# Separate products for two scan steps, folds in four column groups, and a respread schedule in a four-layer selective-scan kernel

## The chip, the cores and the metric

The kernel runs on one core of a Trainium2 chip. The metric is the device time of one launch in microseconds (us). Names of engines: PE is TensorE, DVE is VectorE, ACT is ScalarE, POOL is GpSimd, SP is SyncE, whose queue starts nearly all DMA copies here. The host does no arithmetic; it only rearranges the weights.

## What is computed

Four layers follow each other on x of 8 images, 64 x 64 pixels, 96 channels. Each layer projects up to 2 x 192 channels, convolves, runs a selective scan over the L = 4096 pixels in K directions (4, 4, 4 and 1), sums the directions, gates, and projects down to 96. The scan of a layer is, for every image, direction, channel d and state n (16 of them):

```python
dts, Bs, Cs = jnp.split(x_dbl, ...)            # small projections of u
delta = softplus(dts @ dt_proj_w + bias)
dA = exp(delta * A[d, n])
h  = dA * h + (delta * u) * B[n]               # along the 4096 pixels
y  = sum over n of h * C[n]   ;   y += D * u
```

## The kernel before

**Tiling.** Two images are worked on together: 2 x 192 channels are three tiles (`TILES`) of 128. The sequence is cut into chunks of `CH` = 1024 pixels; a layer has K x 4 x 4 chunks, so 64, 64, 64 and 16, together 208. A chunk has 3 tiles x 16 steps = 48 steps. A step is one scan instruction of 128 partitions x 1024 pixels: the partitions hold 32 channels x 4 states (a "quad"). Two steps are a unit (both halves of 64 channels, same states), four units are a pair of channel groups, eight units are a tile. The loop body (`BODY_CHUNKS` = 2) holds two chunks, 48 units, written out.

**A unit on five engines.** PE spreads the four B rows over the partitions into PSUM (`fill_b`, L897 to L913: two bf16 matmuls with `pick`, into slot 0 alone). DVE multiplies them with du = delta x u (`multiply`, L1046 to L1058: one instruction of 2 x 1024, which reads slot 0 twice and writes both slots), then scans twice (`scan`, L1060 to L1084, decay from SBUF, product from the slot). ACT makes the decays, exp(A x delta), two steps ahead (`decay_of`, L1103), and saves the last state of each unit (`save`, L1125). POOL multiplies both states by C (`gate`, L1274), and PE adds the four states of each channel into `psy` (`reduce`, L970 to L991: four matmuls with the 128 x 32 matrix `fold`). In three units of eight (`POOL_UNITS` = 2, 5, 7) POOL makes the product (`multiply`, L1298, into `made`) and ACT writes the decay into the slot instead; DVE only scans there. I call these P units and the other five m units, so that a tile is m m P m m P m P.

**What a tile needs from elsewhere.** While tile T is scanned, delta and du of tile T + 1 are made. PE projects (`project_delta`), ACT forms the softplus in parts (`parts`, `exponential`, `logarithm`, `correction`), PE sums the four terms (`add_up`), ACT copies the sum into `delta` (`take_delta`, L1168, signal `delta_ready`), and POOL multiplies it by u into `du` (`delta_u`, L1287, signal `du_ready`). SP then spreads both over the partitions, 8 DMA copies of 128 KB for each pair of channel groups (`spread_pair`, L782 to L790), into rings of three (`delta4`) and two (`du4`) buffers. The first product of each tile on DVE waits until all 8 copies of du of the tile's first pair have landed (L1052, L1053).

**The order of the work is written by hand.** Tables of step numbers (L66 to L78) say in which step, counted by n = 0 to 15 in a tile for PE and ACT, or in which unit, 0 to 7, for POOL and SP, each of these jobs stands. Each engine takes its instructions strictly in order, and so does SP's queue (`after_gate`, L807 to L833, and `chunk_work`). In `after_gate` a unit's order on SP is: the y store; in the units that load B or C, a wait for that unit's gate, then 4 copies for C (units 8 to 11 and 20 to 23 of a chunk of 24) and 4 for B (P units); then the spreads whose unit it is. Every chunk is prepared a chunk ahead (`load`, `store_rows`, `load_flat`, `store_split`, `load_bc`). Once a tile ACT copies `psy` to `ybuf` (`copy_y`, L1192) and SP stores it (`store_y`, L798).

Of the kernel before, what the change touches and what calls it, by code (L numbers as in the profile page):

```python
# [60 lines left out]
H_RING, DECAY_RING, DELTA_RING, DU_RING, B_RING, MADE_RING = 4, 3, 3, 2, 2, 2  # L61
AHEAD, REDUCE_LAG = 2, 2
FLAT = 2 * NS * CH // P


DELTA_AT = (0, 1)  # L66
PARTS_AT, EXP_AT, LOG_AT, CORRECTION_AT, TAKE_AT = 2, 3, 4, 5, 8
SUM_AT = (4, 4, 5, 5, 6, 6, 7, 7)
COPY_Y_AT = 4
XDBL_AT = [(0, 10), (0, 10), (0, 11), (0, 12), (0, 13), (0, 14)]  # L70
SAVE_AT = [(0, 12), (0, 15)]
HI_AT, REST_AT, MID_AT, LESS_MID_AT, LO_AT = (1, 9), (1, 10), (1, 11), (1, 12), (1, 13)

DU_AT, Y_STORE = 4, 1
# [525 lines left out]
def scan_stage(nc, kind, T, W, useq, neg_a, yseq, bcdram, splitdram):  # L600
# [29 lines left out]

    def filled(v):

        return v + 1 - sum(w <= v for w in on_pool)

    def by_vector(s):
# [3 lines left out]
    def pair_of(v):  # L639

        return v // QUADS
# [31 lines left out]
    with ExitStack() as ctx:  # L673
# [32 lines left out]
        state = sb("state", [P, 2, TILES * NS])  # L706
        slots = ctx.enter_context(nc.psum_tensor("slots" + W["tag"], [P, 2, CH], F32))
        slot = [slots[:, j, :] for j in range(2)]
        psc = ctx.enter_context(nc.psum_tensor("psc" + W["tag"], [P, CH], F32))
# [19 lines left out]
        with nc.Block() as block:  # L729
            @block.sync  # L730
            def _(sp):
# [65 lines left out]

                def store_y(i, C0, T_):  # L798

                    q, t = T_ // TILES, T_ % TILES  # L800
                    sp.wait_ge(sem["y_copied"], C0 * TILES + (T_ + 2))
                    here = chunk_and_direction(i, q)[0]
                    if backward(q):
                        here = here + SEQS[kind] * PAIRS * NCH
                    sp.dma_start(yseq[here, t], ybuf[:]).then_inc(sem["y_stored"], 16)

                def after_gate(i, C0, v):  # L807
# [24 lines left out]
                    if n == DELTA_OUT_AT[1]:  # L832
                        spread_delta(2 * T_ + 3)  # L833

# [45 lines left out]
                sp.wait_ge(sem["y_stored"], 16 * (NC * TILES + 2))  # L880
                sp.wait_ge(sem["x_full"], 80 * (NC + 1))
# [14 lines left out]
            def _(pe):  # L896
                def fill_b(C0, v, first=False):  # L897

                    body, v = v // BU, v % BU
                    q = v // UNITS  # L900
                    if v in on_pool:
                        return
                    S = (C0 + body * BODY_CHUNKS) * STEPS + 2 * v
                    if v % UNITS == 0:
# [4 lines left out]
                    rows_of = batch_of(v) * QUADS + v % QUADS  # L909
# [26 lines left out]
                def add_up(A, term, a):  # L936


                    if term == 0 and a == 0:
                        pe.wait_ge(sem["relu_ready"], A + 1)  # L940
                        pe.wait_ge(sem["abs_ready"], A + 1)
                    if term == 1 and a == 0:
                        pe.wait_ge(sem["log_ready"], A + 1)
                    if term == 2 and a == 0:
                        pe.wait_ge(sem["excess_ready"], A + 1)
                    if term == 3 and a == 0:
                        pe.wait_ge(sem["exp_ready"], A + 1)
                    mm = pe.matmul(psc[:, HALF[a]], T["ident"][:, :],  # L948
                                   (relu, log, excess, ex)[term][:, HALF[a]], start=(term == 0), stop=(term == 3),
                                   skip_group_check=True)  # L950
                    if term == 3 and a == HALVES - 1:
                        mm.then_inc(sem["summed"], 1)
# [17 lines left out]
                def reduce(C0, v):  # L970
# [6 lines left out]
                    if v % TILE_UNITS == SKIP_AT:  # L977

                        q, t = v // UNITS % BODY_CHUNKS, v // TILE_UNITS % TILES
                        order = slice(None, None, -1) if backward(q) else slice(None)  # L980
                        for cols in HALF:
                            pe.matmul(psy[:, cols], dd[q][:, t, :], u[q][:, t, order][:, cols], start=False, stop=False,  # L982
                                      skip_group_check=True)
                    first = 2 * GROUP * (pair_of(v) % 2)
                    for cols in HALF:
# [24 lines left out]
                pe.wait_ge(sem["pick_in"], 16)  # L1010
                fill_b(0, 0, first=True)
                with pe.Fori(0, NC // BODY_CHUNKS) as i:
                    C0 = i * BODY_CHUNKS
                    for s in range(BS):
                        if s % 2 == 0:
                            fill_b(C0, s // 2 + 1)
                        q, t, n = place(s)
                        after = s // NS + 1
                        if n in DELTA_AT:
                            a = DELTA_AT.index(n)  # L1020
                            if a == 0 and t == 0:
                                psc_free(C0 * TILES + s // NS)
                            if a == 0 and t == 2:
                                pe.wait_ge(sem["split_lo"], C0 + (q + 2))
                            project_delta(C0 + (q + (t > 0)), after // TILES % BODY_CHUNKS, after % TILES, a)
                        for j, at in enumerate(SUM_AT):
# [18 lines left out]
            def _(dve):  # L1045
                def multiply(C0, body, v):  # L1046
# [4 lines left out]
                    j = pair_of(v)  # L1051
                    if v % QUADS == 0 or v % QUADS == 1 and v - 1 in on_pool:  # L1052
# [38 lines left out]
                with dve.Fori(0, G) as g:  # L1091
                    with dve.Fori(0, per_g) as half:
                        body = g * per_g + half
                        C0 = body * BODY_CHUNKS
                        for v in range(BU):
                            if v not in on_pool:
                                multiply(C0, body, v)
                            scan(C0, body, 2 * v, g)
# [3 lines left out]
            def _(act):  # L1102
                def decay_of(i, s):  # L1103
# [15 lines left out]
                    else:  # L1119
                        act.wait_ge(sem["h_ready"], S + (H_START - DECAY_RING + 1))  # L1120
                        dst = decay[s % DECAY_RING][:]
                    act.activation(dst, delta4[j % DELTA_RING][:, s % 2, :], ACT.Exp, scale=na[q][:, k:k + 1])\  # L1122
                        .then_inc(sem["decay_ready"], 1)
# [68 lines left out]
                def copy_y(C0, T_, q):  # L1192
# [3 lines left out]

                    act.wait_ge(sem["y_stored"], C0 * (16 * TILES) + 16 * (T_ + 1))
                    order = slice(None, None, -1) if backward(q) else slice(None)
                    act.copy(ybuf[:], psy[:, order]).then_inc(sem["y_copied"], 1)


                act.sem_inc(sem["state_saved"], H_RING)

                act.sem_inc(sem["y_stored"], 32)

# [648 lines left out]
```

## Time and profile before

| | us |
|---|---|
| median of 3 runs | 35931.14 (35928.1 to 35933.79) |
| the profiled execution | 35929.24 |
| its span in the trace | 35927.5 |
| DVE busy | 32944.5 (92%) |
| POOL busy | 30835.7 (86%) |
| PE busy | 25878.4 (72%) |
| ACT busy | 19018.1 (53%) |

The span is the time from the first to the last instruction of the profiled execution; "busy" is the time in which an engine had an instruction at work. The stretches of lower use in the trace, between the four scans, are the merging and expanding stages of the layers, which the diff leaves as they are. In the times of the trace, us count from the span's start.

### The profile page before, as it was taken

To read this page: it belongs to the slowest core of one execution; us is meant where nothing else is said; L and a number is where in the kernel's file an instruction comes from. 1 tells how busy PE (TensorE), PEld (TensorE's weight loads), DVE (VectorE), ACT (ScalarE), POOL (GpSimd) and SP (SyncE) were. 2 spreads that over 40 slices of the span, in tenths; PEclk is the share of its full clock that TensorE was granted. 3 is DMA by queue.
4 is the path that set the end of the run, shared out by engine and by line. 5 is a ranking of instruction groups with operands and counts; after the bars stand their busy time and mean duration, and the time that the engine had idled before them with its cause. 6 is when DMAs were issued, how large, how long until landed. Compare 5 with 4: busy or idle time off the path is not lost. (4 is left out here: it accounts for less than half of the span.)

```text
span 35927.5 us, 322721 instructions
## 1 busy us (share of the span) xinstructions
PE 25878.4 (72%) x73032; PEld 8083.4 (22%) x73032; DVE 32944.5 (92%) x14881; ACT 19018.1 (53%) x23286; POOL 30835.7 (86%) x7804
## 2 busy tenths in 40 slices
PE   5777777777766777777777766777777777766777
PEld 2222222222222222222222222222222222222224
DVE  5999999999977999999999977999999999976993
ACT  4555555555534555555555534555555555534551
POOL 1999999999961999999999951999999999964994
PEclk7888888888888888888888888888888888887886
DMA  4666666666675666666666675666666666675665
GB/s 154 176 175 175 177 176 178 176 176 176 176 223 168 177 176 175 177 176 179 176 177 178 176 219 167 177 177 175 176 177 176 178 176 176 177 222 181 176 176 149
DMA packets 2423696, 6402.41 MB, mean 178 GB/s; under 512 B 703824, under 2 KB 875728, under 8 KB 2411728
## 3 DMA queue, kind: packets, MB, share of 16 engines
q1 hardware_dynamic: 2421968, 6387.69, 67.0%
q14 instruction: 1659, 13.59, 0.1%
q8 instruction: 69, 1.13, 0.0%
HBM read 2986.75 MB, written 764.47 MB: 104 GB/s over the span
## 5 line engine op out<-in xcount | busy, mean ns | idle before, releaser
L1283 POOL TENSOR_TENSOR h<-h,c 128x2048 f32<-128x2048 f32 x4992 | 20774.7, 4182 | 242.8 <-DVE h L1083 150.5
L1083 DVE TENSOR_TENSOR_SCAN h<-decay,state,slots 128x1024 f32<-128x1024 f32 x6240 | 14306.8, 2335 | 120.4 <-ACT state L1227 9.3
L988 PE MATMUL psy<-h,t_fold 128*32 128x512 f32 x40000 | 10449.2, 672 | 6.1 <-POOL h L1283 5.9
L1122 ACT ACTIVATE decay<-delta,na 128x1024 f32<-128x1024 f32 x6248 | 7115.4, 1146 | 3014.3 <-DVE h L1083 2775.0
L1079 DVE TENSOR_TENSOR_SCAN h<-slots,state,made 128x1024 f32<-128x1024 f32 x3744 | 8551.7, 2327 | 108.3 <-ACT slots L1122 106.1
L1304 POOL TENSOR_TENSOR made<-du,b 128x2048 f32<-128x2048 f32 x1872 | 7823.4, 4179 | 669.4 <-DMA b<-bcdram 669.4
L911 PE MATMUL slots<-bc,pick 96*128 96x512 bf16 x6248 | 2327.4, 461 | 7905.6 <-DVE h L1079 6853.2
L1056 DVE TENSOR_TENSOR slots<-du,slots 128x2048 f32<-128x2048 f32 x3120 | 7165.4, 2297 | 706.9 <-PE slots L911 298.6
L1122 ACT ACTIVATE slots<-delta,na 128x1024 f32<-128x1024 f32 x3744 | 4166.0, 1114 | 5010.9 <-DVE h L1083 5009.4
L988 PEld LDWEIGHTS psy<-h,t_fold 128*32 128x32 f32 x40000 | 2202.4, 120 | 7785.7 <-issue 7522.8
L1296 POOL TENSOR_TENSOR du<-delta,u 128x1024 f32<-128x1024 f32 x628 | 1478.0, 2353 | 2356.3 <-ACT delta L1176 2356.3
L911 PEld LDWEIGHTS slots<-bc,pick 96*128 96x128 bf16 x6248 | 371.4, 101 | 10707.3 <-DVE h L1079 8558.5
L1130 ACT COPY state<-h 128x2 f32<-128x2 f32 x4992 | 923.8, 185 | 2300.2 <-DVE h L1083 1356.7
L948 PE MATMUL psc<-relu,t_ident 128*128 128x512 f32 x2512 | 1932.8, 915 | 9.2 <-ACT ex L1146 9.2
L919 PE MATMUL psc<-u,wx 128*96 128x512 f32 x2544 | 1647.5, 785 | 202.2 <-DMA bdt<-in_bdt 201.2
L982 PE MATMUL psy<-u,dd 128*128 128x512 f32 x2496 | 1758.5, 846 | 0.0
L1176 ACT COPY delta<-psc 128x1024 f32<-128x1024 f32 x628 | 636.5, 1014 | 1567.7 <-PE psc L948 1567.7
L948 PE MATMUL psc<-log,t_ident 128*128 128x512 f32 x2512 | 1414.7, 692 | 51.5 <-ACT log L1159 51.5
L929 PE MATMUL psc<-dts,wdt 32*128 32x512 f32 x2512 | 1436.2, 696 | 0.9 <-ACT dts L1210 0.9
L948 PE MATMUL psc<-excess,t_ident 128*128 128x512 f32 x2512 | 1181.9, 592 | 0.0
L948 PE MATMUL psc<-ex,t_ident 128*128 128x512 f32 x2512 | 1180.4, 592 | 0.0
L1693 POOL TENSOR_TENSOR tn<-tn,zc 128x1536 f32<-128x1536 f32 x96 | 350.9, 3655 | 920.4 <-ACT tn L1572 920.4
(111 smaller groups left out, 20168.8 us busy)
## 6 DMA issues: line engine op xcount, KB each, us to landing
delta<-delta SPq DMA_DIRECT2D x10048, 128.0 KB, 2.6
du<-du SPq DMA_DIRECT2D x10048, 128.0 KB, 3.0
b<-bcdram SPq DMA_DIRECT2D x7520, 128.0 KB, 2.8
c<-bcdram SPq DMA_DIRECT2D x6720, 128.0 KB, 2.9
u<-useq SPq DMA_DIRECT2D x212, 1536.0 KB, 6.9
yseq<-ybuf SPq DMA_DIRECT2D x624, 512.0 KB, 2.7
ya<-yseq SPq DMA_DIRECT2D x420, 512.0 KB, 4.9
yb<-yseq SPq DMA_DIRECT2D x360, 512.0 KB, 5.9
```

The costliest lines, as they stand in the source:

```text
L911: mm = pe.matmul(slot[0][:, cols], pick[:, rows_of, :], bc[q % 2][:, cols], start=True, stop=True)
L919: mm = pe.matmul(psc[0:96, HALF[a]], wx[q][:, s, :], u[q][:, s, HALF[a]], start=(s == 0), stop=(s == TILES - 1))
L948: mm = pe.matmul(psc[:, HALF[a]], T["ident"][:, :], (relu, log, excess, ex)[term][:, HALF[a]], start=(term == 0), stop=(term == 3), skip_g ...
L982: pe.matmul(psy[:, cols], dd[q][:, t, :], u[q][:, t, order][:, cols], start=False, stop=False, skip_group_check=True)
L988: mm = pe.matmul(psy[rows, cols], T["fold"][:, :], h[v % H_RING][:, c, cols], start=(v % QUADS == 0), stop=(v % QUADS == QUADS - 1), skip_ ...
L1056: dve.tensor_tensor(slots[:, ::-1, :], du4[j % DU_RING][:, ::-1, 1:], slots[:, 0:1, :].broadcast_to((P, 2, CH)), ALU.mult)\
L1079: dve.tensor_tensor_scan(out, slot[s % 2][:, order], made[p % MADE_RING][:, s % 2, order], first, ALU.mult, ALU.add).then_inc(sem["h_ready ...
L1083: dve.tensor_tensor_scan(out, decay[s % DECAY_RING][:, order], slot[s % 2][:, order], first, ALU.mult, ALU.add).then_inc(sem["h_ready"], 1)
L1122: act.activation(dst, delta4[j % DELTA_RING][:, s % 2, :], ACT.Exp, scale=na[q][:, k:k + 1])\
L1283: pool.tensor_tensor(both[:, :, 0:CH], both[:, :, 1:], c4[g][:, order].unsqueeze(1).broadcast_to((P, 2, CH)), ALU.mult)\
L1296: pool.tensor_tensor(du[:], delta[:, 1:], u[q][:, t, :], ALU.mult).then_inc(sem["du_ready"], 1)
L1304: pool.tensor_tensor(made[k % MADE_RING][:], du4[j % DU_RING][:, :, 1:], b4[k % B_RING][:].unsqueeze(1).broadcast_to((P, 2, CH)), ALU.mult)\
```

## The change

B is filled into both PSUM slots (two tensors now), two matmuls for each step; DVE makes one product of 1024 for each step, and waits in it only for `b_full` (and du). PE's jobs between the folds stand on odd steps, with the order of the sum's terms changed. The folds of one unit go to four 32-wide column groups: the two halves of the 1024 pixels now lie in different partitions of `psy`, and the two pairs of channel groups in its two banks. `copy_y` and `store_y` follow that layout (two DMA copies in place of one). The sum for delta is taken in step 10 in place of 8, POOL forms du in unit 5 in place of 4, and SP spreads both pairs of delta in unit 4, in front of du (before: the first in unit 3, the second in unit 4 behind du). Later stores and loads of a chunk move by two or three units.

```diff
-DELTA_AT = (0, 1)
-PARTS_AT, EXP_AT, LOG_AT, CORRECTION_AT, TAKE_AT = 2, 3, 4, 5, 8
-SUM_AT = (4, 4, 5, 5, 6, 6, 7, 7)
+DELTA_AT = (1, 1)
+PARTS_AT, EXP_AT, LOG_AT, CORRECTION_AT, TAKE_AT = 2, 3, 4, 5, 10
+SUM_AT = (3, 3, 5, 5, 7, 7, 9, 9)
...
-XDBL_AT = [(0, 10), (0, 10), (0, 11), (0, 12), (0, 13), (0, 14)]
-SAVE_AT = [(0, 12), (0, 15)]
-HI_AT, REST_AT, MID_AT, LESS_MID_AT, LO_AT = (1, 9), (1, 10), (1, 11), (1, 12), (1, 13)
-DU_AT, Y_STORE = 4, 1
+XDBL_AT = [(0, 11), (0, 11), (0, 13), (0, 13), (0, 15), (0, 15)]
+SAVE_AT = [(0, 14), (1, 0)]
+HI_AT, REST_AT, MID_AT, LESS_MID_AT, LO_AT = (1, 10), (1, 11), (1, 12), (1, 13), (1, 14)
+DU_AT, Y_STORE = 5, 1
...
-DELTA_OUT_AT, DU_OUT_AT = (3, 4), (4, 7)
-LOAD_AT, ROWS_STORE_AT, FLAT_AT, SPLIT_STORE_AT, BC_AT = 2, 6, 8, 13, 15
+DELTA_OUT_AT, DU_OUT_AT = (4, 4), (4, 7)
+LOAD_AT, ROWS_STORE_AT, FLAT_AT, SPLIT_STORE_AT, BC_AT = 2, 8, 10, 16, 18
...
+                    if n == DELTA_OUT_AT[0]:
+                        sp.wait_ge(sem["delta_ready"], C0 * TILES + (T_ + 2))
+                        spread_delta(2 * T_ + 2)
+                    if n == DELTA_OUT_AT[1]:
+                        spread_delta(2 * T_ + 3)
                     if n == DU_OUT_AT[0]:
                         sp.wait_ge(sem["du_ready"], C0 * TILES + (T_ + 2))
                         spread_du(2 * T_ + 2)
                     if n == DU_OUT_AT[1]:
                         spread_du(2 * T_ + 3)
-                    if n == DELTA_OUT_AT[0]:
-                        sp.wait_ge(sem["delta_ready"], C0 * TILES + (T_ + 2))
-                        spread_delta(2 * T_ + 2)
-                    if n == DELTA_OUT_AT[1]:
-                        spread_delta(2 * T_ + 3)
...
                     for cols in HALF:
-                        mm = pe.matmul(slot[0][:, cols], pick[:, rows_of, :], bc[q % 2][:, cols],
+                        mm = pe.matmul(slot[s % 2][:, cols], pick[:, rows_of, :], bc[q % 2][:, cols],
                                        start=True, stop=True)
...
-                    first = 2 * GROUP * (pair_of(v) % 2)
-                    for cols in HALF:
+                    bank = HALF[pair_of(v) % 2]
+                    for a, cols in enumerate(HALF):
                         for c in range(2):
-                            rows = slice(first + GROUP * c, first + GROUP * c + GROUP)
-                            mm = pe.matmul(psy[rows, cols], T["fold"][:, :], h[v % H_RING][:, c, cols],
+                            rows = slice(2 * GROUP * a + GROUP * c, 2 * GROUP * a + GROUP * c + GROUP)
+                            mm = pe.matmul(psy[rows, bank], T["fold"][:, :], h[v % H_RING][:, c, cols],
...
                     for s in range(BS):
-                        if s % 2 == 0:
-                            fill_b(C0, s // 2 + 1)
+                        if s % 2 == 1:
+                            fill_b(C0, s - 1 + FILL_LAG)
+                            fill_b(C0, s + FILL_LAG)
...
-                    dve.wait_ge(sem["b_full"], body * filled(BU - 1) + filled(v))
-                    dve.wait_ge(sem["h_ready"], C0 * STEPS + (2 * v + H_START))
...
-                    dve.tensor_tensor(slots[:, ::-1, :], du4[j % DU_RING][:, ::-1, 1:],
-                                      slots[:, 0:1, :].broadcast_to((P, 2, CH)), ALU.mult)\
-                        .then_inc(sem["b_multiplied"], 2)
+                    dve.tensor_tensor(slot[s % 2][:], du4[j % DU_RING][:, s % 2, 1:], slot[s % 2][:], ALU.mult)\
+                        .then_inc(sem["b_multiplied"], 1)
```

## Rows read from the trace of the kernel before

**Rows 1.** The page's costliest groups: those of the scan stages on DVE and POOL
```profile
L1283 POOL TENSOR_TENSOR h<-h,c 128x2048 f32<-128x2048 f32 x4992 | 20774.7, 4182 | 242.8 <-DVE h L1083 150.5
L1083 DVE TENSOR_TENSOR_SCAN h<-decay,state,slots 128x1024 f32<-128x1024 f32 x6240 | 14306.8, 2335 | 120.4 <-ACT state L1227 9.3
...
L1079 DVE TENSOR_TENSOR_SCAN h<-slots,state,made 128x1024 f32<-128x1024 f32 x3744 | 8551.7, 2327 | 108.3 <-ACT slots L1122 106.1
L1304 POOL TENSOR_TENSOR made<-du,b 128x2048 f32<-128x2048 f32 x1872 | 7823.4, 4179 | 669.4 <-DMA b<-bcdram 669.4
...
L1056 DVE TENSOR_TENSOR slots<-du,slots 128x2048 f32<-128x2048 f32 x3120 | 7165.4, 2297 | 706.9 <-PE slots L911 298.6
...
L1296 POOL TENSOR_TENSOR du<-delta,u 128x1024 f32<-128x1024 f32 x628 | 1478.0, 2353 | 2356.3 <-ACT delta L1176 2356.3
```
**Rows 2.** Timeline of DVE over one tile, second of its chunk (start, length, operation, count)
```profile
7032.27 2.30 DVE L1056 TENSOR_TENSOR slots<-du,slots 128x2048 f32<-128x2048 f32 x1 [0.19 <-DVE h L1079]
...
7057.80 2.30 DVE L1056 TENSOR_TENSOR slots<-du,slots 128x2048 f32<-128x2048 f32 x1
7060.13 4.58 DVE L1083 TENSOR_TENSOR_SCAN h<-decay,state,slots 128x1024 f32<-128x1024 f32 x2
7064.63 4.57 DVE L1079 TENSOR_TENSOR_SCAN h<-slots,state,made 128x1024 f32<-128x1024 f32 x2
7069.31 2.30 DVE L1056 TENSOR_TENSOR slots<-du,slots 128x2048 f32<-128x2048 f32 x1
...
7080.90 2.30 DVE L1056 TENSOR_TENSOR slots<-du,slots 128x2048 f32<-128x2048 f32 x1 [0.19 <-DVE h L1079]
```
**Rows 3.** The stages' first and last product on DVE, first and third layer (ns min/median/max)
```profile
L1056 DVE TENSOR_TENSOR slots<-du,slots x960: 2295/2297/2298, 803.2 to 10212.8; 128x2048 f32<-128x2048 f32 x192
...
L1056 DVE TENSOR_TENSOR slots<-du,slots x960: 2295/2297/2298, 22381.8 to 31765.8; 128x2048 f32<-128x2048 f32 x192
```
**Rows 4.** Groups by line and shape: DVE's short products with a PSUM operand
```profile
L1395 DVE TENSOR_TENSOR xr<-xr,outp 96x512 f32<-96x512 f32 x128 | 81.6, 678 | 43.0 <-PE outp L1508 43.0
...
L1395 DVE TENSOR_TENSOR xr<-xr,outp 96x256 f32<-96x256 f32 x128 | 44.9, 410 | 22.9 <-PE outp L1508 22.9
```
**Rows 5.** Timeline of ACT in the tile of rows 2, steps 8 to 11
```profile
7059.61 1.01 ACT L1176 COPY delta<-psc 128x1024 f32<-128x1024 f32 x1 [1.67 <-PE psc L948]
...
7064.75 1.12 ACT L1122 ACTIVATE slots<-delta,na 128x1024 f32<-128x1024 f32 x1 [0.79 <-DVE h L1083]
7065.81 0.18 ACT L1130 COPY state<-h 128x2 f32<-128x2 f32 x1
7065.89 2.25 ACT L1122 ACTIVATE decay<-delta,na 128x1024 f32<-128x1024 f32 x2
```
**Rows 6.** Timeline of SP's queue: the third tile of the chunk before, then the tile of rows 2
```profile
6970.75 1.71 SPq L773 DMA_DIRECT2D c<-bcdram  x4
6972.50 4.95 SPq L788 DMA_DIRECT2D du<-du  x8
...
7065.06 4.96 SPq L788 DMA_DIRECT2D delta<-delta  x8
7070.06 5.03 SPq L788 DMA_DIRECT2D du<-du  x8
7075.14 5.11 SPq L788 DMA_DIRECT2D delta<-delta  x8
```
**Rows 7.** The spreading copies of L788, from issue to landing
```profile
DMA to landing us min/median/max: 2.2/2.8/9.1
```
**Rows 8.** PE around a tile's start (timeline), and all of L929 in 4000 us
```profile
6979.62 1.04 PE L911 MATMUL slots<-bc,pick 96*128 96x512 bf16 x2 [6.93 <-DVE h L1079]
...
6987.21 0.61 PE L911 MATMUL slots<-bc,pick 96*128 96x512 bf16 x2 [1.55 <-DVE h L1083]
6987.75 1.98 PE L929 MATMUL psc<-dts,wdt 32*128 32x512 f32 x4
...
L929 PE MATMUL psc<-dts,wdt x328: 587/588/1217, 5025.2 to 8999.0; 32*128 32x512 f32 x164
```

More of the change, by code:

```diff
@@ L629, in place @@
         return s // STEPS, s // NS % TILES, s % NS
-    def filled(v):
-        return v + 1 - sum(w <= v for w in on_pool)
     def by_vector(s):
@@ L706, in scan_stage @@
         state = sb("state", [P, 2, TILES * NS])
-        slots = ctx.enter_context(nc.psum_tensor("slots" + W["tag"], [P, 2, CH], F32))
-        slot = [slots[:, j, :] for j in range(2)]
+        slot = [ctx.enter_context(nc.psum_tensor(f"slot{j}" + W["tag"], [P, CH], F32)) for j in range(2)]
         psc = ctx.enter_context(nc.psum_tensor("psc" + W["tag"], [P, CH], F32))
@@ L804, in store_y @@
                         here = here + SEQS[kind] * PAIRS * NCH
-                    sp.dma_start(yseq[here, t], ybuf[:]).then_inc(sem["y_stored"], 16)
+                    halves = yseq[here, t].rearrange("(r p) (a f) -> a p r f", r=2, a=HALVES)
+                    for a in range(HALVES):
+                        sp.dma_start(halves[HALVES - 1 - a if backward(q) else a],
+                                     ybuf[2 * GROUP * a:2 * GROUP * a + 2 * GROUP, :].rearrange("p (r f) -> p r f", r=2))\
+                            .then_inc(sem["y_stored"], 16)
                 def after_gate(i, C0, v):
@@ L879, in _ @@
                             chunk_work(i, C0, v)
-                sp.wait_ge(sem["y_stored"], 16 * (NC * TILES + 2))
+                sp.wait_ge(sem["y_stored"], 32 * (NC * TILES + 2))
                 sp.wait_ge(sem["x_full"], 80 * (NC + 1))
@@ L896, in _, with fill_b @@
             def _(pe):
[L897 to L901, printed above, removed]
+                def fill_b(C0, s, first=False):
+                    body, s = s // BS, s % BS
+                    q, t, n = place(s)
+                    if s // 2 in on_pool:
                         return
-                    S = (C0 + body * BODY_CHUNKS) * STEPS + 2 * v
-                    if v % UNITS == 0:
+                    S = (C0 + body * BODY_CHUNKS) * STEPS + s
+                    if t == 0 and n == 0:
                         pe.wait_ge(sem["bc_in"], (C0 + body * BODY_CHUNKS) * 16 + 16 * (q + 1))
@@ L908, in fill_b @@
                         pe.wait_ge(sem["h_ready"], S + (H_START - 1))
-                    rows_of = batch_of(v) * QUADS + v % QUADS
+                    rows_of = batch_of(s // 2) * QUADS + s // 2 % QUADS
                     for cols in HALF:
-                        mm = pe.matmul(slot[0][:, cols], pick[:, rows_of, :], bc[q % 2][:, cols],
+                        mm = pe.matmul(slot[s % 2][:, cols], pick[:, rows_of, :], bc[q % 2][:, cols],
                                        start=True, stop=True)
@@ L942, in add_up @@
                     if term == 1 and a == 0:
+                        pe.wait_ge(sem["exp_ready"], A + 1)
+                    if term == 2 and a == 0:
                         pe.wait_ge(sem["log_ready"], A + 1)
-                    if term == 2 and a == 0:
+                    if term == 3 and a == 0:
                         pe.wait_ge(sem["excess_ready"], A + 1)
-                    if term == 3 and a == 0:
-                        pe.wait_ge(sem["exp_ready"], A + 1)
                     mm = pe.matmul(psc[:, HALF[a]], T["ident"][:, :],
-                                   (relu, log, excess, ex)[term][:, HALF[a]], start=(term == 0), stop=(term == 3),
+                                   (relu, ex, log, excess)[term][:, HALF[a]], start=(term == 0), stop=(term == 3),
                                    skip_group_check=True)
@@ L980, in reduce @@
                         order = slice(None, None, -1) if backward(q) else slice(None)
-                        for cols in HALF:
-                            pe.matmul(psy[:, cols], dd[q][:, t, :], u[q][:, t, order][:, cols], start=False, stop=False,
-                                      skip_group_check=True)
-                    first = 2 * GROUP * (pair_of(v) % 2)
-                    for cols in HALF:
+                        for r in range(2):
+                            chans = slice(2 * GROUP * r, 2 * GROUP * r + 2 * GROUP)
+                            for a, cols in enumerate(HALF):
+                                pe.matmul(psy[2 * GROUP * a:2 * GROUP * a + 2 * GROUP, HALF[r]], dd[q][:, t, chans],
+                                          u[q][:, t, order][:, cols], start=False, stop=False, skip_group_check=True)
+                    bank = HALF[pair_of(v) % 2]
+                    for a, cols in enumerate(HALF):
                         for c in range(2):
-                            rows = slice(first + GROUP * c, first + GROUP * c + GROUP)
-                            mm = pe.matmul(psy[rows, cols], T["fold"][:, :], h[v % H_RING][:, c, cols],
+                            rows = slice(2 * GROUP * a + GROUP * c, 2 * GROUP * a + GROUP * c + GROUP)
+                            mm = pe.matmul(psy[rows, bank], T["fold"][:, :], h[v % H_RING][:, c, cols],
                                            start=(v % QUADS == 0), stop=(v % QUADS == QUADS - 1),
@@ L1010, in _ @@
                 pe.wait_ge(sem["pick_in"], 16)
-                fill_b(0, 0, first=True)
+                for s in range(FILL_LAG):
+                    fill_b(0, s, first=True)
                 with pe.Fori(0, NC // BODY_CHUNKS) as i:
@@ L1014, in _ @@
                     for s in range(BS):
-                        if s % 2 == 0:
-                            fill_b(C0, s // 2 + 1)
+                        if s % 2 == 1:
+                            fill_b(C0, s - 1 + FILL_LAG)
+                            fill_b(C0, s + FILL_LAG)
                         q, t, n = place(s)
                         after = s // NS + 1
[L1019 to L1025, printed above, removed]
+                        for a, at in enumerate(DELTA_AT):
+                            if n == at:
+                                if a == 0 and t == 0:
+                                    psc_free(C0 * TILES + s // NS)
+                                if a == 0 and t == 2:
+                                    pe.wait_ge(sem["split_lo"], C0 + (q + 2))
+                                project_delta(C0 + (q + (t > 0)), after // TILES % BODY_CHUNKS, after % TILES, a)
                         for j, at in enumerate(SUM_AT):
@@ L1045, in _, with multiply @@
             def _(dve):
-                def multiply(C0, body, v):
-                    dve.wait_ge(sem["b_full"], body * filled(BU - 1) + filled(v))
-                    dve.wait_ge(sem["h_ready"], C0 * STEPS + (2 * v + H_START))
-                    j = pair_of(v)
-                    if v % QUADS == 0 or v % QUADS == 1 and v - 1 in on_pool:
+                def multiply(C0, body, s):
+                    q, t, n = place(s)
+                    count = by_vector(s)
+                    dve.wait_ge(sem["b_full"], body * by_vector(BS - 1) + count)
+                    j = pair_of(s // 2)
+                    if s // 2 % QUADS == 0 or s // 2 % QUADS == 1 and s // 2 - 1 in on_pool and s % 2 == 0:
                         dve.wait_ge(du_in[j % DU_RING], body * DU_BODY + du_count(j))
-                    dve.tensor_tensor(slots[:, ::-1, :], du4[j % DU_RING][:, ::-1, 1:],
-                                      slots[:, 0:1, :].broadcast_to((P, 2, CH)), ALU.mult)\
-                        .then_inc(sem["b_multiplied"], 2)
+                    dve.tensor_tensor(slot[s % 2][:], du4[j % DU_RING][:, s % 2, 1:], slot[s % 2][:], ALU.mult)\
+                        .then_inc(sem["b_multiplied"], 1)
                 def scan(C0, body, s, g):
@@ L1096, in _ @@
                             if v not in on_pool:
-                                multiply(C0, body, v)
+                                multiply(C0, body, 2 * v)
+                                multiply(C0, body, 2 * v + 1)
                             scan(C0, body, 2 * v, g)
@@ L1120, in decay_of @@
                         act.wait_ge(sem["h_ready"], S + (H_START - DECAY_RING + 1))
-                        dst = decay[s % DECAY_RING][:]
-                    act.activation(dst, delta4[j % DELTA_RING][:, s % 2, :], ACT.Exp, scale=na[q][:, k:k + 1])\
+                        dst = decay[s % DECAY_RING]
+                    act.activation(dst[:], delta4[j % DELTA_RING][:, s % 2, :], ACT.Exp, scale=na[q][:, k:k + 1])\
                         .then_inc(sem["decay_ready"], 1)
@@ L1195, in copy_y @@
                     act.wait_ge(sem["reduced"], C0 * UNITS + (T_ * TILE_UNITS + H_RING + REDUCE_LAG))
-                    act.wait_ge(sem["y_stored"], C0 * (16 * TILES) + 16 * (T_ + 1))
+                    act.wait_ge(sem["y_stored"], C0 * (32 * TILES) + 32 * (T_ + 1))
                     order = slice(None, None, -1) if backward(q) else slice(None)
-                    act.copy(ybuf[:], psy[:, order]).then_inc(sem["y_copied"], 1)
+                    act.copy(ybuf[:].rearrange("p (r f) -> p r f", r=2),
+                             psy[:].rearrange("p (r f) -> p r f", r=2)[:, :, order]).then_inc(sem["y_copied"], 1)
                 act.sem_inc(sem["state_saved"], H_RING)
-                act.sem_inc(sem["y_stored"], 32)
+                act.sem_inc(sem["y_stored"], 64)
                 act.preload_act_table_set("natural_log_exp_and_others")
```

2 lines of the change are left out of this document (1 added, 1 removed).

## The prediction

> **What bounds the kernel now.** I read first the page's costliest groups, then DVE's timeline over a tile, then what SP's queue, ACT and PE do in that tile. The groups [rows 1] show two engines level in the scans: DVE is busy for 14306.8 + 8551.7 + 7165.4 = 30024 us, POOL for 20774.7 + 7823.4 + 1478.0 = 30076 us. Over 208 x 3 = 624 tiles that is 48.1 and 48.2 us a tile. The first and last product of a scan [rows 3] give the pace: 10212.8 - 803.2, plus 11.6 us for units 6 and 7 behind the last product (7080.90 - 7069.31 in [rows 2]), over 64 chunks is 147.2 us a chunk; the third layer gives 146.8. I take 147.0, or 49.0 us a tile. DVE's idle time stands in front of its products, 706.9 us in all [rows 1], nearly nothing in front of its scans; so DVE is the bound, POOL stands right behind it, and POOL's own largest wait in the loop is for the copies of B.
>
> DVE's idle time is mostly its own. Two scans with no wait between them take 4.58 us for 2 x 2335 ns: the second starts 2.25 us after the first, before the first has ended. A product that waits for the scan in front of it starts 0.10 us late (7064.63 + 4.57 = 7069.20, then 7069.31), and the scan behind a product starts 0.03 us late (7057.80 + 2.30, then 7060.13) [rows 2].
>
> **Part 1: two products for one.** A product of 512 takes 678 ns and one of 256 takes 410 [rows 4], so 1.047 ns an element and some 142 ns fixed. One of 1024 is then 2297 - 1024 x 1.047 = 1225 ns. In the new order no instruction of DVE waits for the one just ahead of it: a scan waits for the product two ahead, a product for `b_full` alone. If products overlap as scans do, by 0.08 us, each costs 1.145 us. A tile is then 10 x 1.145 + 16 x 2.255 = 47.5 us against 49.0: a gain of 1.5 us for DVE, if nothing else stood in the way. A rule speaks against it. The Trainium skill, VectorE: DVE Perf Modes, section on the DRAIN that can't be avoided, says that the next operation doesn't start until the pipeline has emptied, and that semaphores add nothing to that. The scans here disagree with both halves, as the 4.58 us and the 0.10 us above show [rows 2]. Without overlap, a tile is 10 x 1.225 + 16 x 2.335 = 49.6 us; I keep that as the other end.
>
> **Part 2: when delta and du arrive.** This is what decides. Take the tile of [rows 2]. Scan 9, the last of unit 4, ends at 7060.13 + 4.58 = 7064.71. Before, ACT took delta in step 8, at 7059.61, ahead of that scan's end; its late decay(10) stood behind it [rows 5]. Afterwards it takes it in step 10: behind decay(11) and the save of unit 4, which both wait for scan 9, and behind decay(12). These start at 7064.75, 7065.81 and 7065.89; the two decays of the last row take 2.25 us together, so the copy could start at 7066.95 and end 1.01 us later: **3.25 us after scan 9**. (POOL's du, now behind unit 4's gate, is there 4.2 + 2.35 = 6.6 us after scan 9; SP needs it only later.)
>
> SP's queue is then in order: 16 copies of delta, 8 of du. Before, the 8 of du stood in the middle. 24 such copies took 7080.25 - 7065.06 = 15.2 us [rows 6], 0.63 us each, so the last one starts after 14.55 us; it lands 2.8 us later [rows 7]. With 0.1 us for two semaphores, the du of the next tile is there 3.25 + 14.55 + 2.8 + 0.1 = **20.7 us after scan 9**. DVE has 2 x 2.255 + (2 x 1.145 + 2 x 2.255) + 2 x 2.255 = 15.8 us of work until it wants it (before: 7080.90 - 7064.71 = 16.2 us, with du landed at 7070.06 + 4.4 + 2.8 = 7077.3, 3.6 us early). So DVE stands still for about 4.9 us at every tile's first product.
>
> This is a closed ring, so no buffer evens it out: first product, units 0 to 4 (8 x 1.145 + 10 x 2.255 + 0.1 = 31.8 us; before, 7064.71 - 7032.27 = 32.4), then the 20.7 us: **52.5 us a tile**, over DVE's 47.5 and POOL's 48.2.
>
> In a chunk's third tile SP's unit 4 begins with 4 copies of C that wait for the gate of unit 4, 4.2 us after scan 9 (4182 ns, [rows 1]), and take 1.7 us [rows 6]. Delta starts at 5.9 in place of 3.25: **2.7 us more once a chunk**.
>
> **Part 3: PE and ACT at a tile's start.** Before, delta's projection stood behind the fill that waits for scan 0. Now it stands behind the fill that waits for scan 1. PE has two levels: two fills take 0.61 us at the upper (2.4 GHz) and 1.04 us at the lower one (1.2 GHz), the latter after 6.9 us of idle time, and the projection 1.98 us, or twice that (588 to 1217 ns for one record) [rows 8]. At the upper level ACT gets it 0.05 + 0.45 + 1.85 = 2.35 us after scan 1. Relu and Abs (2.1 us) are through at 4.5, decay(4) then waits for scan 2 as before, ends at 5.7, the exponentials run to 7.7, decay(5) to 8.8, and DVE wants it at 2 x 1.145 + 3 x 2.255 = 9.05: no cost. At the lower level the projection is there at 4.5, decay(4) at 7.7 where scan 4 is due at 6.8, decay(5) at 10.8 where it is due at 10.0: 1.8 us in all, and it lies in the ring. DVE's standstill leaves PE without work for some 4 us ahead of this, which makes the lower level as likely as not. I take **1.0 us**, between 0 and 1.8. The fill of slot 1 has only one product as its cover (1.07 us against 0.05 + 1.04): 0.1 us at most, counted at nothing.
>
> **Part 4: the rest.** The folds become cheaper if four column groups work at once, the fills dearer by two matmuls; both hide beside DVE, since PE is idle for a quarter of the span (72% busy on the page). The second y store is one more issue on SP in unit 1, far from unit 4. Moving the x projection frees ACT and DVE of a wait of at most the 106.1 us in all that L1079 waits for ACT [rows 1], and the standstill swallows that. Copies of B for P units stand behind du; they land about 2.6 us into the next tile and POOL's product is needed 13.6 us into it: nothing.
>
> **The sum.** A chunk is 3 x (52.5 + 1.0) + 2.7 = 163.2 us against 147.0, so 16.2 us more; 208 chunks make 3370 us. On the profiled execution of 35929 us that gives 39,300; the median of the runs is 2 us off it.
>
> **Bounds.** Low: no PE term, every copy 0.62 us and the last landing after 2.2: 51.65 us a tile, 157.7 a chunk, 38,150. High: no overlap on DVE (33.5 for 31.8), landing after 3.0, the PE term in full: 56.2 us, 171.4 a chunk, 41,000. All at their high end together is unlikely, so I go to 40,500.
>
> **Rivals.** (1) *Faster:* SP's queue isn't the bound. The 0.63 us for a spreading copy would have to fall to about the 0.43 of a C copy (1.71 us for 4, [rows 6]), since DVE's own pace spreads traffic; then 24 copies take 10.2 us, the ring is 31.8 + 3.25 + 9.8 + 2.8 + 0.1 = 47.75 us and POOL's 48.2 decides. The ring decides from 48.2 us on, that is from 0.45 us a copy. A chunk would be some 146, with a little of POOL's wait for B left: 1 us x 208 gained, **35,720**. Against it: the same copies took 0.62 to 0.64 us each in all four runs of 8 in [rows 6], whatever stood around them. (2) *The fixed cost of a product:* the ring doesn't bind and instructions don't overlap; by the rule above a tile is 49.6 + 10 x 0.03 = 49.9, so 0.9 x 624 = 560 us: **36,490**. It needs the ring's absence too, and the scans speak against the rest. (3) *The folds don't run four at a time,* so that the change doesn't do what it says on PE: 0.85 us a unit of PE time is not gained, and the time stays at my forecast, since nothing waits for it.
>
> **How the numbers follow.** The ring of delta and du sets the pace: 0.91 (with it (3), which has no time of its own). Rival (1), or DVE's gain by another road: 0.05. Rival (2): 0.03. No net effect: 0.01. A difference below 0.2%, 72 us, can't be told from none. Faster 0.05, same 0.01, slower 0.94. The range is the ring's own, cut at the unlikely high end: 38,100 to 40,500.
>
> **What would show it.** Right: DVE's idle time before its products rises from 707 us to some 3,000 or more, one long wait of 4 to 8 us a tile, released by the DMA copies of du; products of about 1225 ns, starting 1.15 us apart; POOL's busy time as before and its waits for DVE's scans much longer; a C, delta, du sequence on SP with no gap in unit 4, delta's first copy 3.3 us after scan 9. Part 3 shows in waits of scans in P unit 2 for ACT. Wrong: tiles under 50 us, du landed before scan 15 ends, or POOL with hardly any idle time.

## The result and the profile after

The changed kernel takes 39814.79 us (median of 4, 39807.08 to 39822.37) against 35932.46 for the kernel before, a ratio of 1.1078 (95% interval 1.1064 to 1.1091). The forecast was 39,300 in a range of 38,100 to 40,500.

DVE's waits over the whole span, from the list of waits (in total, times, longest):

```profile
DVE slot L1062 <- DMA du<-du: 3531.6, 620, 8.8
DVE h L1084 <- ACT slot L1128: 1123.6, 1241, 1.4
...
DVE slot L1062 <- PE slot L911: 250.3, 4, 62.9
```

Before, the largest of DVE's waits in the scan stages came to some 300 us (for fills), of which some 250 lie at the starts of the four stages, as the third line still does (4 times, up to 62.9 us). Now one wait, for du, stands at 620 of 624 tiles and costs 5.7 us each time; a second, of scans in P units for ACT, costs 1.8 us a tile. The costliest groups of the page that answer to [rows 1]:

```profile
L1290 POOL TENSOR_TENSOR h<-h,c 128x2048 f32<-128x2048 f32 x4992 | 20787.4, 4176 | 3358.8 <-DVE h L1088 1892.0
L1088 DVE TENSOR_TENSOR_SCAN h<-decay,state,slot 128x1024 f32<-128x1024 f32 x6240 | 14286.5, 2332 | 0.0
...
L1062 DVE TENSOR_TENSOR slot<-du,slot 128x1024 f32<-128x1024 f32 x6240 | 7427.1, 1217 | 3788.2 <-DMA du<-du 3531.6
...
L1084 DVE TENSOR_TENSOR_SCAN h<-slot,state,made 128x1024 f32<-128x1024 f32 x3744 | 8632.4, 2334 | 1124.4 <-ACT slot L1128 1123.6
...
L991 PE MATMUL psy<-h,t_fold 128*32 128x512 f32 x40000 | 6478.8, 731 | 4.1 <-POOL h L1290 4.1
```

The work itself cost hardly more: products 7427 us busy for 7165, scans as before, folds 6479 for 10449, and DVE is busy for 32816 us in all, for 32945 before. What grew is idle time: 3788 us before DVE's products, 3359 before POOL's gates. DVE's timeline from one standstill to the next, the second tile of a chunk and the start of the third, to be read beside [rows 2]:

```profile
6990.26 2.36 DVE L1062 TENSOR_TENSOR slot<-du,slot 128x1024 f32<-128x1024 f32 x2 [4.78 <-DMA du<-du]
...
7004.67 2.35 DVE L1084 TENSOR_TENSOR_SCAN h<-slot,state,made 128x1024 f32<-128x1024 f32 x1 [0.83 <-ACT slot L1128]
7007.50 2.35 DVE L1084 TENSOR_TENSOR_SCAN h<-slot,state,made 128x1024 f32<-128x1024 f32 x1 [0.47 <-ACT slot L1128]
...
7018.75 4.58 DVE L1088 TENSOR_TENSOR_SCAN h<-decay,state,slot 128x1024 f32<-128x1024 f32 x2
7023.24 4.57 DVE L1084 TENSOR_TENSOR_SCAN h<-slot,state,made 128x1024 f32<-128x1024 f32 x2
...
7043.97 2.36 DVE L1062 TENSOR_TENSOR slot<-du,slot 128x1024 f32<-128x1024 f32 x2 [4.83 <-DMA du<-du]
```

Scan 9 ends at 7018.75 + 4.58 = 7023.33 and the next tile begins at 7043.97, 20.6 us later. The same stretch on ACT and then on SP's queue:

```profile
7024.50 1.14 ACT L1128 ACTIVATE decay<-delta,na 128x1024 f32<-128x1024 f32 x1
7025.55 0.39 ACT L1188 CAST split<-flat 128x256 bf16<-128x256 f32 x1
7025.85 1.00 ACT L1182 COPY delta<-psc 128x1024 f32<-128x1024 f32 x1
```
```profile
7026.87 10.21 SPq L783 DMA_DIRECT2D delta<-delta  x16
7037.13 5.04 SPq L783 DMA_DIRECT2D du<-du  x8
...
7081.99 1.71 SPq L768 DMA_DIRECT2D c<-bcdram  x4
7083.80 10.44 SPq L783 DMA_DIRECT2D delta<-delta  x16
7094.29 5.16 SPq L783 DMA_DIRECT2D du<-du  x8
```

Delta is ready 3.5 us after scan 9, the queue then issues 24 copies without a gap, and du, whose own product was long done, comes last. The last three lines are the third tile: C first, then the same, and the next tile starts at 7101.25, 57.3 us after 7043.97 (the tile before: 53.7 us). Over all tiles of the trace the means are 54.2 us for the first, 54.2 for the second and 57.1 for the third of a chunk, 165.6 us a chunk for the 163.2 of the forecast.

PE at the start of that third tile, for the second wait. In front of these lines it had been idle for 3.8 and 1.2 us:

```profile
7048.64 0.61 PE L911 MATMUL slot<-bc,pick 96*128 96x512 bf16 x2 [4.47 <-DVE h L1088]
7050.88 1.03 PE L911 MATMUL slot<-bc,pick 96*128 96x512 bf16 x2 [1.63 <-DVE h L1088]
7051.84 3.77 PE L929 MATMUL psc<-dts,wdt 32*128 32x512 f32 x4
```

The projection takes 3.77 us, for 1.98 in [rows 8]: it runs at PE's lower level.

### The profile page after: what moved, and what is told of

It reads as the page before. It is cut to its first block and busy times, and to the rows that moved or that the text cites. A ratio compares the mean times of both kernels' runs of the same rounds, so it can differ in the third digit from the quotient of the medians.

```text
span 39805.3 us, 347905 instructions
## 1 busy us (share of the span) xinstructions
PE 26392.7 (66%) x81776; PEld 7265.3 (18%) x81776; DVE 32816.2 (82%) x18001; ACT 18826.1 (47%) x23286; POOL 30911.6 (78%) x7804
## 5 line engine op out<-in xcount | busy, mean ns | idle before, releaser
L1088 DVE TENSOR_TENSOR_SCAN h<-decay,state,slot 128x1024 f32<-128x1024 f32 x6240 | 14286.5, 2332 | 0.0
L911 PE MATMUL slot<-bc,pick 96*128 96x512 bf16 x12496 | 4999.0, 492 | 11231.8 <-DVE h L1084 5800.3
L1062 DVE TENSOR_TENSOR slot<-du,slot 128x1024 f32<-128x1024 f32 x6240 | 7427.1, 1217 | 3788.2 <-DMA du<-du 3531.6
L1084 DVE TENSOR_TENSOR_SCAN h<-slot,state,made 128x1024 f32<-128x1024 f32 x3744 | 8632.4, 2334 | 1124.4 <-ACT slot L1128 1123.6
L1128 ACT ACTIVATE slot<-delta,na 128x1024 f32<-128x1024 f32 x3744 | 4177.1, 1116 | 6427.4 <-DVE h L1088 6427.4
L991 PE MATMUL psy<-h,t_fold 128*32 128x512 f32 x40000 | 6478.8, 731 | 4.1 <-POOL h L1290 4.1
L929 PE MATMUL psc<-dts,wdt 32*128 32x512 f32 x2512 | 2339.8, 1082 | 0.9 <-ACT dts L1217 0.9
L984 PE MATMUL psy<-u,dd 128*64 128x512 f32 x4992 | 1897.6, 903 | 0.0
L991 PEld LDWEIGHTS psy<-h,t_fold 128*32 128x32 f32 x40000 | 895.8, 120 | 4969.4 <-issue 4393.3
L565 DVE SCALAR_TENSOR_TENSOR acc<-xp,convw,acc 128x4096 f32<-128x4096 f32 x240 | 1074.0, 4478 | 3.3
```

The source lines that it names most:

```text
L911: mm = pe.matmul(slot[s % 2][:, cols], pick[:, rows_of, :], bc[q % 2][:, cols], start=True, stop=True)
L929: pe.matmul(psc[:, HALF[a]], wdt[q][:, t, :], dts[q][:, HALF[a]], start=True, stop=True)\
L984: pe.matmul(psy[2 * GROUP * a:2 * GROUP * a + 2 * GROUP, HALF[r]], dd[q][:, t, chans], u[q][:, t, order][:, cols], start=False, stop=False ...
L991: mm = pe.matmul(psy[rows, bank], T["fold"][:, :], h[v % H_RING][:, c, cols], start=(v % QUADS == 0), stop=(v % QUADS == QUADS - 1), skip_ ...
L1062: dve.tensor_tensor(slot[s % 2][:], du4[j % DU_RING][:, s % 2, 1:], slot[s % 2][:], ALU.mult)\
L1084: dve.tensor_tensor_scan(out, slot[s % 2][:, order], made[p % MADE_RING][:, s % 2, order], first, ALU.mult, ALU.add).then_inc(sem["h_ready ...
```

## The experiments

All are timed against the kernel before on the same chip; "ratio" is to that kernel. Each is an edit of the changed kernel unless it says otherwise. The diffs are abridged: of a table of step numbers only what differs is shown, and where code is moved, its sense.

**e1: the late schedule alone, on the kernel before.**

```diff
-TAKE_AT = 8   DU_AT = 4   DELTA_OUT_AT = (3, 4)
+TAKE_AT = 10  DU_AT = 5   DELTA_OUT_AT = (4, 4), both deltas ahead of du
+XDBL_AT = [(0, 11), (0, 11), (0, 12), (0, 13), (0, 14), (0, 15)]
+SAVE_AT, HI_AT to LO_AT, ROWS_STORE_AT to BC_AT as in the change
```

> The kernel before with the late schedule alone: delta taken in step 10, du formed in unit 5, both deltas spread in unit 4 ahead of du, the x projection, the split and the chunk's stores moved as in the change; one product for both steps, the old folds. Theory (the ring first product, scan 9, delta, 24 copies, du landed): 32.4 + 20.7 = 53.1 us a tile, 2.7 more in a chunk's third tile, 162.0 us a chunk against 147.0, so about 39,070 us, with DVE waiting for du at nearly every tile. Rival (the two products and their fixed cost are what costs): 35,930, as before.

Measured: 39009.68, ratio 1.0854 (1.0823 to 1.0886). The old product waits exactly as the new ones do:

```profile
7048.69 2.29 DVE L1056 TENSOR_TENSOR slots<-du,slots 128x2048 f32<-128x2048 f32 x1 [4.62 <-DMA du<-du]
...
7104.37 2.29 DVE L1056 TENSOR_TENSOR slots<-du,slots 128x2048 f32<-128x2048 f32 x1 [7.25 <-DMA du<-du]
```

So 3,073 of the 3,882 us come with the schedule and without a second product. The rival of the products' fixed cost falls. The second wait is not there: scans in P units wait 0.0 us in all. Delta's projection is at PE's lower level here too (1093 ns a record in the mean), but it stands behind the fill that waits for scan 0, not for scan 1, and begins at 7054.39, before scan 1 ends at 7055.61.

**e2: du between the two deltas on SP.**

```diff
+                    spread_delta(2 * T_ + 2)
+                    wait du_ready; spread_du(2 * T_ + 2)
+                    spread_delta(2 * T_ + 3)
-                    spread_delta(2 * T_ + 2); spread_delta(2 * T_ + 3)
-                    wait du_ready; spread_du(2 * T_ + 2)
```

> The changed kernel, but in unit 4 SP spreads the first pair of delta, then du, then the second pair of delta (the order of before). Theory: du's 8 copies start 3.25 + 5.1 = 8.35 us after scan 9 and the last lands at 15.7, just when DVE wants it (15.8). A tile falls to 31.8 + 1.8 + 15.8 = 49.4, the third of a chunk to 52.1: 150.9 us a chunk, 36,750 us. Rival (the copies are slow because there are many of them, in any order; or the products cost it): 39,800.

Measured: 36618.20, ratio 1.0189 (1.0159 to 1.0219). The same copies in another order, and 3,197 us are gone. The waits for du fall from 620 to 208, one a chunk, where the C copies stand in front (636 us in all). What is left, 681 us over the kernel before, goes with these waits, with those for ACT (362 us) and with those for fills (535 us, of which 250 at the stages' starts), less what DVE gains by the products.

**e3: delta and du early, the order on SP kept.**

```diff
-TAKE_AT = 10  DU_AT = 5  SUM_AT = (3, 3, 5, 5, 7, 7, 9, 9)
+TAKE_AT = 8   DU_AT = 4  SUM_AT = (3, 3, 5, 5, 5, 5, 7, 7)
```

> The changed kernel with delta taken in step 8 and du formed in unit 4 (the sum's terms in steps 3, 5, 5 and 7), while SP keeps 16 copies of delta ahead of du in unit 4. Theory: du lands about 15.3 us after scan 9 in a chunk's first two tiles, 49.4 us each; in the third, SP's unit 4 still begins with C copies that wait for the gate of unit 4, so it keeps its 57.0. A chunk is 155.8 us, about 37,780 us. Rival (the order of the copies alone is at fault, not the time at which delta is taken): 39,800.

Measured: 38166.15, ratio 1.0620 (1.0589 to 1.0651): 1,649 us gained of the 2,035 expected. The third tile's standstill is longer than I said:

```profile
7080.11 2.37 POOL L1303 TENSOR_TENSOR du<-delta,u 128x1024 f32<-128x1024 f32 x1
7082.41 4.19 POOL L1290 TENSOR_TENSOR h<-h,c 128x2048 f32<-128x2048 f32 x1
```
```profile
7106.19 2.36 DVE L1062 TENSOR_TENSOR slot<-du,slot 128x1024 f32<-128x1024 f32 x2 [9.25 <-DMA du<-du]
```

Scan 9 ends at 7081.13 here, but POOL is still at du, so the gate of unit 4, for which the C copies wait, ends 5.5 us after it and not 4.2. But this does not explain the miss: over all tiles the third takes 57.3 us in the mean, for the 57.0 expected, because the tile's first part became shorter. The miss lies mostly in the second tile, 50.6 us for 49.4 (the first: 49.8). There too SP stands at C copies, those for the gate of unit 3, so that delta, taken early, goes out only 1.1 us after scan 9 (7024.49 + 4.58 = 7029.07):

```profile
7028.34 1.69 SPq L768 DMA_DIRECT2D c<-bcdram  x4
7030.15 10.09 SPq L783 DMA_DIRECT2D delta<-delta  x16
```

Of the 447 waits for du, 239 stand elsewhere than behind the third tile. Time and order each matter; neither alone is the cause.

**e4: delta's projection in step 0.**

```diff
-DELTA_AT = (1, 1)
+DELTA_AT = (0, 0)
```

> The changed kernel with delta's projection in step 0 in place of step 1, so that PE does it without waiting for scan 1. Theory: the 1124 us that scans of P units wait for ACT vanish, 1.8 us a tile inside the ring; 39,815 - 1,120 = about 38,690 us, the waits for du as long as before. Rival (those waits lie beside the wait for du and cost nothing by themselves): 39,800, with the waits for du longer by as much.

Measured: 38575.53, ratio 1.0734 (1.0703 to 1.0765): 1,239 us gained, while the waits for du stay at 3515.7 us. The wait for ACT lay in the ring and was paid in full; the 115 us more than its 1,124 are not explained. From a tile's first product to the end of scan 9 DVE now takes 31.7 us in the mean, for 33.7 in the changed kernel and 32.5 in e1.

**e5: the old folds.** The folds, the skip product, the layout of `psy`, `copy_y` and the single y store of before.

> The changed kernel with the folds, the skip product, the layout of psy and the single y store of before (two column groups a unit, 1.9 us of PE time for a unit's folds in place of 1.06). Theory: folds are on no path; what could change is PE's clock in front of delta's projection: busier, PE may hold the upper level there, and the 1.8 us a tile for which scans wait for ACT shrink. Between 38,700 (all of it) and 39,815 (none). Rival (the four column groups are a gain of their own): slower than 39,815.

Measured: 39843.23, ratio 1.1089 (1.1066 to 1.1111): as the change, 28 us above the upper end of what I expected, which is within the noise. The projection's records keep a median of 1056 ns, the lower level, as in the change. Scans now wait 285 us for ACT and 878 us for folds in `psy` that stand behind the projection, together 1,163 us for 1,124: another releaser, the same delay. The second DVE wait is not the folds. That it is the projection's place e4 shows; that it is PE's level too, the runs with the projection in step 1 show together. By the mean of its records, 1082 ns in the change, 901 in e3, 775 in e2 and 648 in e6, DVE waits for ACT 1124, 661, 362 and 72 us.

**e6: the change with the times and the order of before.** e3 and, on SP, the first delta pair in unit 3, then du, then the second pair in unit 4.

> The changed kernel (two products, four column groups) with the times of before for the ring: delta taken in step 8, du in unit 4, first delta pair in unit 3, du and then the second delta pair in unit 4. Theory: du lands in time, DVE needs 47.5 us a tile plus some 0.5 to 1.8 for ACT in the first P unit; POOL needs 48.2 and waits for B as before, about 2.7 us a chunk: 147 to 148 us a chunk, 35,900 to 36,150 us. Rival (DVE alone was the bound before, and its 1.5 us a tile come through): 35,000 us.

Measured: 35835.44, ratio 0.9973 (0.9963 to 0.9983). The whole loss is gone, though two products, the four column groups, PE's odd steps and the chunk's later stores are all still there: none of them carries it. The time is 65 us under the range that I expected, and the gain left, 100 us or 0.16 us a tile, is a fraction of DVE's 1.5. Busy times in a stretch of 1000 us inside a scan, before and then e6 (PE, PE's weight loads, DVE, ACT, POOL, each with its count; then PE's granted clock, the DMA share, GB/s):

```profile
6000.00:7000.00 1000.00, 736.85 (x2103) 215.29 (x2102) 976.77 (x429) 563.67 (x702) 973.15 (x245) 0.84 0.69 175
```
```profile
6000.00:7000.00 1000.00, 685.23 (x2406) 180.71 (x2405) 973.55 (x533) 560.86 (x702) 978.12 (x247) 0.79 0.71 178
```

POOL now is the busier one, and it waits for B as before (672 us). DVE waits 724 us for fills, 474 without the stages' starts.

**e7 and e8: the projection in step 0, on e6 and on e2.**

> As e6, and delta's projection in step 0. Theory: the wait for ACT goes; DVE then needs 47.5 us a tile and POOL, 48.2 and its waits for B, sets the pace: 146 to 147 us a chunk, 35,700 to 35,950 us, so at best 0.6% under the kernel before. Rival (as in e6): 35,000 us.

> The changed kernel with du spread between the two delta pairs and delta's projection in step 0; delta still taken in step 10, du in unit 5. Theory: e2's 36,618 less what of the waits for ACT (362 us) and for the fills (about 280 us) was in the ring, while the third tile's wait for du stays (636 us): 36,250 to 36,500 us. Rival (the residue of e2 is the products' own cost): 36,618.

Measured: e7 36611.09, ratio 1.0189 (1.0172 to 1.0206); e8 37316.11, ratio 1.0386 (1.0368 to 1.0403). In both the sign of my expectation was wrong: what gave 1,239 us in e4 costs 776 and 698 here. PE at a tile's start in e7, then DVE:

```profile
7018.43 1.98 PE L929 MATMUL psc<-dts,wdt 32*128 32x512 f32 x4
7020.34 1.04 PE L911 MATMUL slot<-bc,pick 96*128 96x512 bf16 x4
```
```profile
7020.98 2.36 DVE L1062 TENSOR_TENSOR slot<-du,slot 128x1024 f32<-128x1024 f32 x2 [0.99 <-PE slot L911]
```

PE comes to step 0 late, behind the skip product and the folds of unit 7's step, and the projection then stands in front of both fills for unit 1. DVE's waits for fills go from 724 to 1705 us; in e8 they are 1375 us, for 535 in e2, and its waits for POOL's products 479, for 163. In e4 DVE begins each tile some 5 us late, and it waits for fills at the four stages' starts alone (251 us).

**e9: the second delta pair in unit 6, on e6.** `DELTA_OUT_AT = (3, 6)` in place of (3, 4).

> As e6, but the second delta pair is spread in unit 6 in place of 4, so that SP reaches the B copies of unit 5 some 5 us earlier in a chunk's third tile. Theory (in e6 POOL is the bound: 979 of 1000 us busy, and 672 us of waiting for B): that wait shrinks to the 124 us of the stages' starts, and 200 to 500 us come off e6's 35,835: 35,350 to 35,650 us. Rival (DVE's waits for the fills, 724 us, bound e6): 35,835 unchanged.

Measured: 35438.59, ratio 0.9864 (0.9849 to 0.9879), as expected: 397 us under e6. POOL's group that makes the products:

```profile
L1311 POOL TENSOR_TENSOR made<-du,b 128x2048 f32<-128x2048 f32 x1872 | 7822.9, 4179 | 123.4 <-DMA b<-bcdram 123.4
```

**e10: the same move on the kernel before.**

> The kernel before with the same single move, the second delta pair in unit 6. Theory (before, DVE is the bound, and POOL's wait for B lies beside it): POOL's wait shrinks, the time stays within 0.2% of 35,935 us. Rival (POOL and DVE were level, and both bound it): 100 to 400 us faster.

Measured: 35802.99, ratio 0.9965 (0.9952 to 0.9979). The wait for B falls from 669 to 124 us, and 122 us come off. The theory said at most 0.2%, 72 us, and the rival 100 to 400: the rival holds. DVE was the bound only most of the time.

**e11 and e12: the old folds on e6 and on e9.**

> e6 with the folds, the layout of psy and the single y store of before. Theory: PE has 0.85 us more to do in each unit, so the second fill of a unit comes later, and it has only one product as its cover: DVE's waits for fills (724 us in e6) grow by 0.2 to 1 us in some of the five units, 100 to 1,000 us: 35,950 to 36,800 us. Rival (the folds are on no path here either): 35,835.

> e9 with the folds, the layout of psy and the single y store of before. Theory (the two gains add up: PE at the upper level more of the time, as in e11 against e6, 116 us; and the second delta pair in unit 6, as in e9 against e6, 397 us): about 35,320 us. Rival (with DVE and POOL 0.99 busy there is nothing left for the clock to give): 35,440.

Measured: e11 35719.47, ratio 0.9943 (0.9927 to 0.9958), 116 us under e6 (the two intervals do not touch), where I expected 100 to 1,000 over it. e12 35260.44, ratio **0.9817** (0.9803 to 0.9830), for an expected 35,320: the fastest of all. The two windows that answer to those above, e11 and then e12:

```profile
6000.00:7000.00 1000.00, 766.26 (x2332) 214.58 (x2333) 975.63 (x536) 569.50 (x711) 981.92 (x248) 0.88 0.70 178
```
```profile
6000.00:7000.00 1000.00, 773.90 (x2367) 216.09 (x2364) 988.22 (x543) 570.98 (x716) 996.34 (x251) 0.88 0.69 180
```

With the old folds PE is busier (766 us for 685) and its granted clock higher (0.88 for 0.79); DVE's waits for fills fall from 724 to 523 us. Between e9 and e12 they hardly move (522 and 498 us) while the time falls by 178; there DVE's waits for ACT go from 97 to 4 us and POOL's for DVE's scans from 286 to 120. In e12 POOL is busy 996 of 1000 us.

## Why the prediction was right, and where it was off

**The bound of before.** DVE first and POOL right behind: right for most of the time. Of the 707 us in front of DVE's products, which were to show it, some 250 lie at the starts of the four stages. That POOL's wait for B lies beside DVE's work, as I still expected for e10, was wrong by 122 us.

**Part 1, the products.** 1217 ns each for a forecast 1225. In some 60% of the pairs the second starts 1.11 to 1.14 us after the first, as the 2.33 and 2.36 us above say; in 40% (2.44 us) it starts 1.20 to 1.22 us after, without overlap, and why is open. From the start of a pair to that of the next scan it is 2.29 us in the mean, just the forecast's 2 x 1.145. As for the rule weighed there: the Trainium skill, VectorE: DVE Perf Modes, section The DRAIN you can't avoid, itself adds that a next operation that is not held starts earlier, so it was no argument against the overlap, which scans and most products show. DVE's gain is real but was hidden. Where both kernels stand in the same ring it is plain: from a tile's first product to scan 9 DVE takes 31.7 us in e4 for 32.5 in e1, and e4 is 434 us faster, 0.7 us a tile. Without the ring, e12 is 543 us under e10, 0.87 us a tile: what the products bring together with the PE schedule on odd steps, once POOL's wait for B and the new folds are out of the way. POOL, at 996 of 1000 us, keeps the rest.

**Part 2, the ring.** 20.6 us from scan 9 to the next tile for a forecast 20.7; delta ready after 3.5 for 3.25, which a shorter landing (2.5 us in the median of du, for 2.8) takes back; a standstill of 4.8 us in front of the second and third tile (forecast 4.9) and 7.7 behind the third (7.6). e1 had 39,010 for an expected 39,070, e2 36,618 for 36,750. This step is shown: it comes without the products (e1) and goes with the order of the copies alone (e2).

**Part 3, PE and ACT at a tile's start.** The mechanism was right, the size was off: 1,124 us, 1.8 us a tile, for the 1.0 I took. That is its upper end, split as 1.4 and 0.5 us where the working has 0.9 and 0.8 (which add up to 1.7, not 1.8). PE was at the lower level not every second time but nearly always: the projection's records take 1056 ns in the median for 588 in [rows 8], and 97% of them over 1000. 0.8 x 624 = 500 us is nearly the whole difference between 39,300 and 39,815. By e4 the term is 2.0 us a tile; what that adds, copies and landing took back, with 20.4 to 20.7 us from scan 9 to the next tile for 20.7.

**Part 4.** The folds became cheaper as said (6479 us for 10449), and at the changed kernel's pace that is worth nothing (e5). That the kernel can be faster with the old folds (e11, e12) was not in it. The copies of B, counted at nothing, came later: POOL's waits for them went from 669 to 1326 us. In the changed kernel that cost nothing, since no scan of DVE waits for POOL's product; in e6 and before, where POOL is level with DVE, such waits did cost (e9, e10).

**Rivals.** The faster one needed copies at 0.45 us; they kept 0.63 to 0.65 (10.21 for 16, 5.16 for 8). The fixed-cost one fell with e1.

**Open.** e12 against e10 holds the products, the odd-step schedule on PE and the chunk's later stores together; they were not parted. Nor were the parts of the old folds in e11 and e12: with the folds go the skip product (4 matmuls for 8), the layout that ACT copies and one y store for two. Why the copies of delta and du take 0.63 us to issue and those of C 0.43 wasn't tried.

## What to carry to other kernels

Where a result is made, copied and spread one tile ahead, write down its ring: from the first use, through the step in which it is taken, through every copy that the queue holds in front of it, to its landing. As long as that is shorter than the tile it costs nothing; past it, each microsecond is paid once a tile, and moving a small job by two steps or changing the order of two copies decides it. Then look at the second engine: with two engines as level as DVE and POOL here (48.1 and 48.2 us of work a tile), most of a gain on one shows only after the other's waits are removed.

## What was not expected of the hardware

- **The kernels with less work on PE are the slower ones.** Folds in four column groups take 1.06 us a unit for 1.91, but with them PE's granted clock is 0.79 for 0.88, the fills' mean is 468 ns for 443, and the time is 116 us (e6, e11) and 178 us (e9, e12) longer. That the clock is the cause, through PE's short jobs on a path, fits these numbers but is not shown: the y stores and the skip product change along with the folds.
- **With a standstill of DVE, PE projects at its lower level.** Where DVE stands still some 5 us at a tile's start, the projection's records are 1082 ns (the change) and 1093 ns (e1) in the mean; without the standstill, in the same places, 648 ns (e6) and 696 ns (the kernel before).
- **The value of a move changes sign with the bound.** The projection in step 0 gave 1,239 us where DVE stood still at each tile's start and cost 776 us where it didn't.
